# Mixing of the spectra in layer 4: one matmul per mode, real and imaginary weights side by side, in all eight PSUM banks

## Chip, cores and metric

The kernel runs on one core of a Trainium2 chip. The metric is the device time in microseconds (us) of one execution, lower is better. Three runs of the kernel before took 3917.05, 3924.25 and 3925.5 us; their median is 3924.25 us.

## The reference

Four layers are applied to x of shape (8, 32, 128, 128), batch by channel by height by width; each adds its result to its input after a per-plane normalisation `_gn`. The change is in the last layer, which multiplies a global transform by a 3x3 convolution with wrapped borders:

```
c_ft = rfft2(c)
top = einsum('bixy,ioxy->boxy', c_ft[:, :, :16, :16], w1)     # w1 = w1r + 1j*w1i
bot = einsum('bixy,ioxy->boxy', c_ft[:, :, -16:, :16], w2)    # w2 = w2r + 1j*w2i
out_ft = zeros; out_ft[:, :, :16, :16] = top; out_ft[:, :, -16:, :16] = bot
g = irfft2(out_ft);  l = conv3x3(c, wrap) + conv_b;  result = g * l
```

For each of the 512 kept modes (32 rows x by 16 columns y) there is a complex 32 by 32 matrix that turns the 32 input channels of each of 8 images into 32 output channels. This step is called the mixing here.

## The kernel before

Layers 1 to 3 fill most of the time, and the change leaves their work alone; only two semaphores of layer 1's batch norm (`bn_var`, `bn_sd`) are folded into two others with the same order of waits. Layer 4 is worked through image by image (index t, 0 to 7), each engine having its own list of instructions and waiting on counters of the others. For image t, ACT normalises, PE does the transform over rows (`dft_rows`, L789) and over columns (`dft_columns`, L801), ACT copies the spectrum from PSUM to the tile `cs` (`spectrum`, L1073, three copies: minus the imaginary part, the real part, the imaginary part), DVE transposes the image into bands (L1542) and PE convolves them (`conv`, L591, two halves per image of 288 PE matmuls each, into PSUM banks 0 to 3), and ACT copies the convolution out (`conv3_out`, L1080). Each float32 matmul of the program is two weight loads and two matmuls in the profile.

In `cs` and in the weight tile `wm`, partition quadrant q (32 partitions, one for each input channel) holds the modes with x = 4q to 4q+3 of either half of the spectrum. `mix_spectrum` (L857 to L868) does two matmuls per mode, each with 32 rows, 32 weight columns and 16 moving columns: the real weights times (real, imaginary), and the imaginary weights times (minus imaginary, real), added up in PSUM. Quadrant q of the input goes to quadrant q of PSUM, and `grp = (turn + q) % 4` gives the four quadrants a different one of the banks 4 to 7 at any time. There are 1024 such matmuls. The weights come by 16 DMAs of SP (L500), issued before the last image's bands are ready.

After `mix_spectrum` one count of `spec_mm` releases ACT, which copies the result out in 8 instructions (L1127) to the tile `ys`. PE meanwhile goes on with the convolution of the last image. SP waits for all 8 copies, stores `ys` by 8 DMAs (L545) and loads it back, transposed, by one (L548). After the last convolution half has been copied out, the final loop begins: for each image, a slice copy (ACT, L1135), the inverse transforms (PE, L887 and L898, with ACT's L1140 between), and DVE's product and sum (L1580, L1582); SP loads x and the convolution for it (L504, L311) and stores the result (L557). In SP's list `bands_out` (L488) stores a convolution half, `l3_in` and `x3_in` load for the final loop. Buffers for three images are there; the loads of the first three x and first two convolutions are issued before the mixing's results are waited for.

Of the kernel before, what the change touches and what calls it, by code (L numbers as in the profile page):

```python
# [7 lines left out]
ALU = mybir.AluOpType  # L8
ACT = mybir.ActivationFunctionType
AX = mybir.AxisListType  # L10

B, C, H, W = 8, 32, 128, 128
P = 128
# [8 lines left out]
NPX = CR * W  # L22
# [4 lines left out]
MODES = 16  # L27
KX = 2 * MODES
# [65 lines left out]
def after(eng, sem, n):  # L94

    if n > 0:
        eng.wait_ge(sem, n)


def four_layers(nc, x, conv0_w, conv0_b, bn_gamma, bn_beta, filt_x, filt_y, conv1_w, mix1_w, conv1_b, op_rows,  # L100
# [29 lines left out]
    with ExitStack() as ctx:  # L130
        def sb(name, shape, dt=F32):
            return ctx.enter_context(nc.sbuf_tensor(name, shape, dt))

        def once(name):

            return ctx.enter_context(nc.semaphore(name))
# [12 lines left out]
        k = sb("k", [P, NCONST])  # L149
# [17 lines left out]
        sd = sb("sd", [P, C])  # L167
        root = sb("root", [P, C])
        rstd = sb("rstd", [P, 4, C])
        nmr = sb("nmr", [P, 4, C])  # L170
        powers = sb("powers", [P, C])
# [17 lines left out]
        dog = sb("dog", [P, W + 2])  # L189
        cs = sb("cs", [P, 3, 2, 4, MODES, B])  # L190
        ps = ctx.enter_context(nc.psum_tensor("ps", [P, 8, NPX], F32))

        def part(at, n, rows=P):
            return arena[0:rows, at:at + n]
# [36 lines left out]

        wm = part(8192, 4 * C * 64).rearrange("p (r t o m) -> p r t o m", r=2, t=2, o=C)
        ys = part(37512, 2048).rearrange("p (a b m) -> p a b m", a=8, b=B)
# [30 lines left out]
        x_loaded, y_stored = two("x_loaded"), two("y_stored")  # L264
        bn_dev, bn_mat, bn_var, bn_sd, bn_ready = (once(n) for n in ("bn_dev", "bn_mat", "bn_var", "bn_sd", "bn_ready"))

# [21 lines left out]

        wm_loaded, spec_mm, spec_copy, spec_stored, spec_loaded = (once(n) for n in ("wm_loaded", "spec_mm", "spec_copy", "spec_stored", "spec_loaded"))
        xe_loaded, le_loaded, out_stored = ([sem(f"{n}{i}") for i in range(3)] for n in ("xe_loaded", "le_loaded", "out_stored"))  # L290
# [16 lines left out]
        def _(sp):  # L307
# [185 lines left out]
            def weights_in():  # L493

                sp.wait_ge(x3_stored[(B - 2) % 3], 16 * ((B - 2) // 3 + 1))
                sp.wait_ge(bands_ready, B - 1)
                sp.wait_ge(dfth_mm, 4 * (B - 1))
                for r, t, w in ((0, 0, w1r), (1, 0, w1i), (0, 1, w2r), (1, 1, w2i)):
                    for q in range(4):
                        sp.dma_start(wm[C * q:C * q + C, r, t, :, :],  # L500
                                     w[:, :, 4 * q:4 * q + 4, :].rearrange("i o x y -> i o (x y)")).then_inc(wm_loaded, 16)
# [38 lines left out]

            sp.wait_ge(spec_copy, 8)
            for t in range(2):
                for q in range(4):
                    first = MODES * t + 4 * q
                    sp.dma_start(spec_dram[first:first + 4].rearrange("x o m -> o x m"),  # L545
                                 ys[C * q:C * q + C, 4 * t:4 * t + 4, :, :].rearrange("p x b m -> p x (b m)")).then_inc(spec_stored, 16)
# [21 lines left out]
        def _(pe):  # L568
# [223 lines left out]
            def dft_columns(t):  # L792

                pe.wait_ge(dfth_copy, 4 * (t + 1))
                after(pe, dftw_copy, 3 * t)
                for half in range(2):
                    for xx in range(4):
                        for q in range(4):
                            for r in range(2):
                                at = 256 + (4 * half + xx) * 2 * MODES  # L800
                                m = pe.matmul(ps[C * q:C * q + C, 4, at:at + 2 * MODES], z[:, :, r, MODES * half + 4 * q + xx],  # L801
                                              dftw[:, r, :], start=r == 0, stop=r == 1)
                m.then_inc(dftw_mm, 1)
# [24 lines left out]
            for t in range(-2, B + 1):  # L828
# [5 lines left out]
                if 0 <= t < B:  # L834
                    after(pe, dftw_copy, 3 * t)
                    group_means(gn3, t)
# [21 lines left out]
            def mix_spectrum():  # L858

                for turn in range(4):  # L860
                    for m_ in range(KX):
                        for q in range(4):
                            grp = (turn + q) % 4
                            x8, ky = 2 * grp + m_ // MODES, m_ % MODES
                            t, xx = divmod(x8, 4)
                            for r in range(2):
                                m = pe.matmul(ps[C * q:C * q + C, 4 + grp, 16 * m_:16 * m_ + 16], wm[C * q:C * q + C, r, t, :, xx * MODES + ky],  # L867
                                              cs[C * q:C * q + C, 1 - r:3 - r, t, xx, ky, :], start=r == 0, stop=r == 1)  # L868
                m.then_inc(spec_mm, 1)

            pe.wait_ge(wm_loaded, 16 * 16)
            pe.wait_ge(dftw_copy, 3 * B)
            mix_spectrum()
            for half in range(HALVES):
                conv3(B - 1, half, range(TAPS))
# [26 lines left out]
        def _(act):  # L902
# [165 lines left out]
            def spectrum(t):  # L1068

                act.wait_ge(dftw_mm, t + 1)  # L1070
                sp_ = ps[:, 4, 256:256 + 8 * 2 * MODES].rearrange("p (x r y) -> p r x y", x=8, r=2)
                for n, (r, sign) in enumerate(((1, -1.0), (0, 1.0), (1, 1.0))):
                    nc.scalar.activation(cs[:, n, :, :, :, t:t + 1].rearrange("p t x y b -> p (t x) (y b)"),  # L1073
                                         sp_[:, r, :, :], ACT.Copy, scale=sign).then_inc(dftw_copy, 1)

# [47 lines left out]

            act.wait_ge(spec_mm, 1)
            for n in range(8):
                src = ps[:, 4 + n // 2, 256 * (n % 2):256 * (n % 2) + 256].rearrange("p (y r b) -> p b r y", y=MODES, r=2)
                nc.scalar.copy(ys[:, n, :, :].rearrange("p b (r y) -> p b r y", r=2), src).then_inc(spec_copy, 1)  # L1127

            for half in range(HALVES):
                conv3_out(B - 1, half)  # L1130
            act.wait_ge(spec_loaded, 16)
            act.wait_ge(spec_copy, 8)
            with act.Fori(0, B) as b:
# [14 lines left out]
        def _(pool):  # L1148
# [8 lines left out]
            for b in range(B):  # L1157
                pool.wait_ge(gn0.shifted, b + 1)
                nc.gpsimd.tensor_tensor(col0[:, 3:4], col0[:, 3:4], powers[:, 0:1], ALU.pow).then_inc(gn0.root, 1)  # L1159
            pool.wait_ge(bn_var, 1)  # L1160
            nc.gpsimd.tensor_tensor(root[:, :], sd[:, :], powers[:, :], ALU.pow).then_inc(bn_sd, 1)

# [57 lines left out]
        def _(dve):  # L1220
# [177 lines left out]
            t.inc(nc.vector.tensor_copy(bn_m[:, :], ps[:, 1, 0:2 * C]))  # L1398
            nc.vector.tensor_scalar(sd[:, :], ps[:, 1, C:2 * C], BN_EPS, None, ALU.add).then_inc(bn_var, 1)
            dve.wait_ge(bn_sd, 1)  # L1400
            t.inc(nc.vector.tensor_tensor(bn_a[:, :], root[:, :], gam[:, 0:C], ALU.mult))
# [144 lines left out]
            for i in range(-2, B):  # L1546
# [19 lines left out]
                if i >= 0:  # L1566
                    bands(i)

            for b in range(B):
                x3, l3 = xe[b % 3], le[b % 3]  # L1570
# [107 lines left out]
```

## Time and profile before

| | |
|---|---|
| profiled execution: time, and its span | 3922.26 us, 3920.1 us |
| median of three runs | 3924.25 us |
| PE busy, weight loads busy | 3338.9 us (85%), 1184.0 us (30%) |
| DVE, ACT, POOL busy | 2855.7 us (73%), 1849.5 us (47%), 2341.5 us (60%) |
| mean granted TensorE clock | 0.924 |
| chain that ended last | PE 30%, POOL 29%, issue 28%, DVE 5%, ACT 4%, DMA 2% |

The span runs from the first to the last instruction; the time of the execution has some 2 us around it. A stretch is named by its two ends in us from the span's start. In a list of instructions in order of time a row has start, duration, engine, line and operation, the tiles written and read, the shape, a count, and in brackets the idle time before it and what ended it. "Issue" is time in which an engine waited for nothing that the profile shows. Layer 4's images end and the mixing begins at 3640 us; the final loop begins at 3744 us.

### The profile page before, as it was taken

What the parts mean: (1) busy time and instruction counts of PE and PEld (TensorE: products, weight loads), DVE (VectorE), ACT (ScalarE), POOL (GpSimd) and SP (SyncE); (2) the same over time, 40 slices, a digit from 0 to 9 for tenths busy, and PEclk for the clock granted to TensorE, in tenths of its full rate; (3) what the DMA queues carried; (4) which work ended last, traced back from release to release, by engine and by line L of the source; (5) the groups of instructions that cost most, each with busy time, mean ns of one, the idle gap of its engine ahead of it and who ended that gap; (6) DMA issues with size and microseconds to landing.
All of it is one profiled execution on the core that took longest, in us unless ns stands there. A gap on an engine that the chain in (4) does not pass through costs nothing.

```text
span 3920.1 us, 89862 instructions
## 1 busy us (share of the span) xinstructions
PE 3338.9 (85%) x32900; PEld 1184.0 (30%) x32900; DVE 2855.7 (73%) x3513; ACT 1849.5 (47%) x2702; POOL 2341.5 (60%) x1131
## 2 busy tenths in 40 slices
PE   4678999759999999999999999999999957787565
PEld 2343444312212212222222222222222245555454
DVE  3652544469989989989989989989999956655034
ACT  0114566355545545555555555555555455665011
POOL 0000000049999999999999999999999923321000
PEclk9899999879999999999999999999999967888665
DMA  6574898566656656666666666666666664535589
GB/s 158 120 167 99 164 196 169 124 164 155 154 133 148 153 139 145 158 141 144 150 149 143 145 152 147 141 149 151 141 149 159 141 152 118 154 101 128 140 191 251
DMA packets 495204, 586.47 MB, mean 150 GB/s; under 512 B 71970, under 2 KB 334754, under 8 KB 489435
## 3 DMA queue, kind: packets, MB, share of 16 engines
q1 hardware_dynamic: 484212, 563.65, 62.5%
q10 hardware_dynamic: 10560, 16.93, 1.8%
q8 instruction: 287, 4.70, 0.5%
q14 instruction: 145, 1.19, 0.1%
HBM read 409.91 MB, written 184.54 MB: 152 GB/s over the span
## 4 chain that ended last, share of the span: by engine, by line
PE 30%; POOL 29%; issue 28%; DVE 5%; ACT 4%; DMA 2%; SPq 1%; ACTq 0%; POOLq 0%; DVEq 0%
POOL arena L1183 27%; PE ps L591 8%; PE ps L632 7%; PE ps L639 4%; PE ps L703 3%; POOL arena L1171 2%; ACT arena L936 2%; PE ps L789 1%; PE ps L811 1%; DVE arena L1542 1%; PE ps L685 1%; PE ps L898 1%; PE ps L867 1%; DMA arena<-x_dram 1%; DMA w_conv<-in_conv_w 1%
## 5 line engine op out<-in xcount | busy, mean ns | idle before, releaser
L1183 POOL TENSOR_TENSOR arena<-arena 128x1024 f32<-128x1024 f32 x896 | 1931.0, 2196 | 556.2 <-ACT arena L1039 556.2
L1494 DVE TENSOR_TENSOR arena<-ps,arena 128x1024 f32<-128x1024 f32 x1792 | 2107.4, 1220 | 204.9 <-PE ps L685 174.3
L703 PE MATMUL ps<-arena,w_mix 128*32 128x512 f32 x10752 | 1438.5, 607 | 79.4 <-POOL arena L1183 79.4
L1039 ACT ACTIVATE arena<-ps 128x1024 f32<-128x1024 f32 x896 | 918.9, 1026 | 1026.3 <-PE ps L695 1015.3
L685 PE MATMUL ps<-arena,sel 48*128 48x512 bf16 x3584 | 702.5, 385 | 24.8 <-issue 16.1
L685 PEld LDWEIGHTS ps<-arena,sel 48*128 48x128 bf16 x3584 | 190.1, 93 | 945.5 <-issue 936.8
L591 PE MATMUL ps<-arena,w_conv 32*32 32x512 f32 x9216 | 354.0, 650 | 42.6 <-issue 34.3
L695 PE MATMUL ps<-norms,opw 57*128 57x512 bf16 x1792 | 348.1, 384 | 49.2 <-ACT arena L971 17.5
L703 PEld LDWEIGHTS ps<-arena,w_mix 128*32 128x32 f32 x10752 | 214.3, 108 | 467.5 <-issue 467.5
L936 ACT ACTIVATE arena<-arena,nmr,rstd 128x128 f32<-128x128 f32 x768 | 300.5, 481 | 33.0 <-DVE arena L1544 30.4
L632 PE MATMUL ps<-arena,circ 128*128 128x512 f32 x640 | 287.9, 595 | 14.1 <-ACT arena L950 14.1
L695 PEld LDWEIGHTS ps<-norms,opw 57*128 57x128 bf16 x1792 | 101.8, 93 | 435.3 <-issue 430.0
L591 PEld LDWEIGHTS ps<-arena,w_conv 32*32 32x32 f32 x9216 | 179.1, 107 | 178.8 <-issue 125.5
L1215 POOL COPY arena<-arena 32x130 f32<-32x130 f32 x32 | 33.8, 1057 | 327.7 <-DVE arena L1544 326.7
L1166 POOL TENSOR_TENSOR arena<-arena 128x1024 f32<-128x1024 f32 x62 | 133.0, 2145 | 95.7 <-ACT arena L980 95.7
L1580 DVE TENSOR_TENSOR arena<-arena,ps 128x512 f32<-128x512 f32 x64 | 43.7, 683 | 192.7 <-PE ps L898 163.3
L639 PE MATMUL ps<-arena,circ 128*128 128x512 f32 x384 | 176.3, 594 | 0.0
L632 PEld LDWEIGHTS ps<-arena,circ 128*128 128x128 f32 x640 | 120.3, 189 | 166.6 <-issue 166.6
L1226 DVE BATCH_NORM_STATS2 st<-arena 128x6 f32<-128x128 f32 x768 | 156.5, 278 | 7.1 <-POOL arena L1202 4.9
L1422 DVE TENSOR_TENSOR arena<-arena 128x512 f32<-128x512 f32 x64 | 44.3, 692 | 143.1 <-ACT arena L955 141.1
L1159 POOL TENSOR_TENSOR col<-col,powers 128x1 f32<-128x1 f32 x8 | 4.4, 549 | 241.1 <-DVE col L1282 241.1
L811 PE MATMUL ps<-arena,ident 128*128 128x128 f32 x512 | 78.8, 319 | 70.0 <-ACT arena L936 69.9
(151 smaller groups left out, 2195.2 us busy)
## 6 DMA issues: line engine op xcount, KB each, us to landing
arena<-pad SPq DMA_DIRECT2D x768, 260.0 KB, 7.7
split_dram<-arena SPq DMA_DIRECT2D x64, 768.0 KB, 3.6
arena<-split_dram SPq DMA_DIRECT2D x1536, 32.0 KB, 3.2
x_dram<-arena SPq DMA_DIRECT2D x16, 2048.0 KB, 7.8
l_dram<-arena SPq DMA_DIRECT2D x128, 256.0 KB, 4.2
arena<-l_dram SPq DMA_DIRECT2D x32, 1024.0 KB, 14.1
arena<-x_dram SPq DMA_DIRECT2D x16, 2048.0 KB, 16.4
pad<-arena SPq DMA_DIRECT2D x8, 2080.0 KB, 16.4
```

The lines of the kernel that those rows point to most:

```text
L591: m = pe.matmul(ps[C * j:C * j + C, bank + g, :], weights[C * g:C * g + C, dy, dx, :], tile[C * g:C * g + C, r:r + CR, dx:dx + W], start=t ...
L632: m = pe.matmul(ps[:, n % 2, :], circ[:, d, :], yp[h % 2][:, 4 * n:4 * n + 4, 4 - d:4 - d + W], start=d == 0, stop=d == 4)
L639: m = pe.matmul(ps[:, 2 + n % 2, :], circ[:, 5 + d, :], yp[h % 2][:, 4 * n:4 * n + 4, 4 - d:4 - d + W], start=d == 0, stop=d == 2)
L685: m = pe.matmul(ps[:, 2 * (n % 2) + e, :], sel[ROWS2 * e:ROWS2 * e + SPLIT_ROWS, u % GROUP, :], split[ROWS2 * e:ROWS2 * e + SPLIT_ROWS, pa ...
L695: m = pe.matmul(ps[:, POOL_BANK + e, :], opw[ROWS2 * e:ROWS2 * e + KROWS, SPREAD[c], :], norms[ROWS2 * e:ROWS2 * e + KROWS, buf, half, :]. ...
L703: m = pe.matmul(ps[C * g:C * g + C, SUM + chunk % 2, :], w_mix[:, s, :], ring[:, (first + g // 2) % size, NPX * (g % 2):NPX * (g % 2) + NP ...
L936: m = nc.scalar.activation(tile[:, c, :], src[:, c, :], ACT.Identity, scale=rstd[:, gn.slot + n % 2, c:c + 1], bias=nmr[:, gn.slot + n % 2 ...
L1039: nc.scalar.activation(ring_p[:, slot, :], ps[:, POOL_BANK:POOL_BANK + 2, :].rearrange("p a n -> p (a n)"), ACT.Tanh).then_inc(tanh_p, 1)
L1166: nc.gpsimd.tensor_tensor(rest, tt, hml[:, 0, :], ALU.subtract).then_inc(rows_r, 1)
L1183: nc.gpsimd.tensor_tensor(slot, slot, pixels(chunk % 2, SPREAD[n // 2], n % 2), ALU.mult).then_inc(prod_p, 1)
L1226: m = nc.vector.bn_stats(st[:, c, :], tile[:, c, :])
L1494: nc.vector.tensor_tensor(slot, weights, pixels(par, ONCE[n // 2], n % 2), ALU.mult).then_inc(prod_d, 1)
```

## The change

Each mode gets one matmul: 32 rows, 64 weight columns (32 real, 32 imaginary, beside each other in `wm`), 16 moving columns (real and imaginary of 8 images). So 512 matmuls instead of 1024. The results are products, not yet combined: in a PSUM region of 64 partitions the lower 32 hold real weight times (real, imaginary), the upper 32 imaginary weight times the same. Quadrants 0 and 1 of the input go to partitions 0 to 63 and 64 to 127 of bank grp, quadrants 2 and 3 to those of bank 4+grp, so that all eight banks are filled. PE therefore waits for the evacuation of the convolution before (`conv3_evac` 14) ahead of the mixing, and for all combinations (`spec_copy` 4) behind it, ahead of the last image's convolution. The modes are done in four groups (quarters), with one count of `spec_mm` each. A quarter behind, ACT copies the imaginary-weight half to a new tile `crossed` (four copies of 32 partitions by 512 per group), and DVE combines it with the real-weight half from PSUM (eight instructions of 32 partitions by 256 elements per group) into `ys`. SP stores the first half of the spectrum after two groups, the second after four. `cs` loses its negated part, so that `spectrum` is two copies for each image.

```diff
-        cs = sb("cs", [P, 3, 2, 4, MODES, B])
+        cs = sb("cs", [P, 2, 2, 4, MODES, B])
+        crossed = sb("crossed", [P, 2, NPX])
-        wm = part(8192, 4 * C * 64).rearrange("p (r t o m) -> p r t o m", r=2, t=2, o=C)
+        wm = part(8192, 4 * C * 64).rearrange("p (t k m) -> p t k m", t=2, k=2 * C)
@@ SP @@
-                        sp.dma_start(wm[C * q:C * q + C, r, t, :, :],
+                        sp.dma_start(wm[C * q:C * q + C, t, C * r:C * r + C, :],
-            sp.wait_ge(spec_copy, 8)
             for t in range(2):
+                sp.wait_ge(spec_copy, 2 * t + 2)
                 for q in range(4):
@@ PE (dftw_copy is waited for at 2 * t instead of 3 * t) @@
-                for turn in range(4):
+                for grp in range(4):
                     for m_ in range(KX):
+                        x8, ky = 2 * grp + m_ // MODES, m_ % MODES
+                        t, xx = divmod(x8, 4)
                         for q in range(4):
-                            grp = (turn + q) % 4
-                            x8, ky = 2 * grp + m_ // MODES, m_ % MODES
-                            t, xx = divmod(x8, 4)
-                            for r in range(2):
-                                m = pe.matmul(ps[C * q:C * q + C, 4 + grp, 16 * m_:16 * m_ + 16], wm[C * q:C * q + C, r, t, :, xx * MODES + ky],
-                                              cs[C * q:C * q + C, 1 - r:3 - r, t, xx, ky, :], start=r == 0, stop=r == 1)
-                m.then_inc(spec_mm, 1)
+                            rows, at = slice(C * q, C * q + C), 2 * C * (q % 2)
+                            m = pe.matmul(ps[at:at + 2 * C, 4 * (q // 2) + grp, 16 * m_:16 * m_ + 16], wm[rows, t, :, xx * MODES + ky],
+                                          cs[rows, :, t, xx, ky, :], start=True, stop=True)
+                    m.then_inc(spec_mm, 1)
             pe.wait_ge(wm_loaded, 16 * 16)
-            pe.wait_ge(dftw_copy, 3 * B)
+            pe.wait_ge(dftw_copy, 2 * B)
+            pe.wait_ge(conv3_evac, 2 * (B - 1))
             mix_spectrum()
+            pe.wait_ge(spec_copy, 4)
             for half in range(HALVES):
                 conv3(B - 1, half, range(TAPS))
@@ ACT @@
-                for n, (r, sign) in enumerate(((1, -1.0), (0, 1.0), (1, 1.0))):
-                    nc.scalar.activation(cs[:, n, :, :, :, t:t + 1].rearrange("p t x y b -> p (t x) (y b)"),
-                                         sp_[:, r, :, :], ACT.Copy, scale=sign).then_inc(dftw_copy, 1)
+                for r in range(2):
+                    nc.scalar.activation(cs[:, r, :, :, :, t:t + 1].rearrange("p t x y b -> p (t x) (y b)"),
+                                         sp_[:, r, :, :], ACT.Copy).then_inc(dftw_copy, 1)
-            act.wait_ge(spec_mm, 1)
-            for n in range(8):
-                src = ps[:, 4 + n // 2, 256 * (n % 2):256 * (n % 2) + 256].rearrange("p (y r b) -> p b r y", y=MODES, r=2)
-                nc.scalar.copy(ys[:, n, :, :].rearrange("p b (r y) -> p b r y", r=2), src).then_inc(spec_copy, 1)
+            for grp in range(4):
+                act.wait_ge(spec_mm, grp + 1)
+                after(act, spec_copy, grp - 1)
+                for q in range(4):
+                    at = 2 * C * (q % 2) + C
+                    m = nc.scalar.copy(crossed[C * q:C * q + C, grp % 2, :], ps[at:at + C, 4 * (q // 2) + grp, :])
+                m.then_inc(spec_cross, 1)
             act.wait_ge(spec_loaded, 16)
-            act.wait_ge(spec_copy, 8)
@@ DVE, behind its work for the images and ahead of the final loop @@
+            for grp in range(4):
+                dve.wait_ge(spec_cross, grp + 1)
+                for q in range(4):
+                    at = 2 * C * (q % 2)
+                    real, imag = (tile.rearrange("p (x y r b) -> p r x b y", x=2, r=2, b=B)
+                                  for tile in (ps[at:at + C, 4 * (q // 2) + grp, :], crossed[C * q:C * q + C, grp % 2, :]))
+                    own = ys[C * q:C * q + C, 2 * grp:2 * grp + 2, :, :]
+                    nc.vector.tensor_tensor(own[:, :, :, 0:MODES], real[:, 0], imag[:, 1], ALU.subtract)
+                    m = nc.vector.tensor_tensor(own[:, :, :, MODES:KX], real[:, 1], imag[:, 0], ALU.add)
+                m.then_inc(spec_copy, 1)
```

Not shown: the renamed semaphores of layer 1, where POOL waits for `gn0.shifted` and DVE for `gn0.root` instead of `bn_var` and `bn_sd`.

## Rows read from the trace of the kernel before

**Rows 1.** Engines by stretch: length, busy us (count) of each, granted clock, DMA share, GB/s.

```profile
core 0: us, PE busy (x) PEld busy (x) DVE busy (x) ACT busy (x) POOL busy (x), PEclk, DMA share, GB/s
3650.00:3700.00 50.00, 20.18 (x1271) 19.11 (x1264) 0.00 (x0) 0.00 (x0) 0.00 (x0) 0.50 0.55 178
...
3840.00:3860.00 20.00, 14.48 (x192) 12.94 (x192) 9.16 (x15) 3.07 (x5) 0.00 (x0) 0.50 1.12 288
```

**Rows 2.** The chain that ended last, 3636 to 3752, its shares by line.

```profile
by line: issue 40.1%; PE ps L867 28.4%; PE ps L591 23.1%; PE ps L887 5.7%; ACT arena L1080 2.0%; ACT arena L1135 0.8%; ACTq L1133 0.1%; ACTq L1135 0.1%; ACTq L1137 0.0%; ACTq L1138 0.0%
```

**Rows 3.** Instructions in order of time, PE and its weight loads in the mixing.

```profile
3639.90 0.43 PEld L867 LDWEIGHTS ps<-cs,arena 32*32 32x32 f32 x9
...
3640.64 1.18 PEld L867 LDWEIGHTS ps<-cs,arena 32*32 32x32 f32 x69 [0.30 <-issue]
...
3648.28 2.05 PE L867 MATMUL ps<-cs,arena 32*32 32x16 f32 x128 [6.36 <-issue]
...
3657.78 2.05 PE L867 MATMUL ps<-cs,arena 32*32 32x16 f32 x128 [7.45 <-issue]
...
3679.89 2.05 PE L867 MATMUL ps<-cs,arena 32*32 32x16 f32 x128 [1.70 <-issue]
...
3687.10 2.05 PE L867 MATMUL ps<-cs,arena 32*32 32x16 f32 x128 [1.70 <-issue]
...
3716.51 0.83 PE L867 MATMUL ps<-cs,arena 32*32 32x16 f32 x43 [1.42 <-issue]
...
3717.29 11.42 PE L591 MATMUL ps<-arena,w_conv 32*32 32x512 f32 x280
```

**Rows 4.** DMA queues, 3676 to 3719: packets, MB, share of 16 engines.

```profile
q8 instruction: 12, 0.20, 2.0%
```

**Rows 5.** All instructions of L867: form, count, ns min/median/max, first and last start.

```profile
L867 PE MATMUL ps<-cs,arena x2048: 173/212/237, 3639.9 to 3717.3; 32*32 32x16 f32 x187
```

**Rows 6.** Instructions in order of time, on both sides of the mixing.

```profile
3606.95 5.58 PE L591 MATMUL ps<-arena,w_conv 32*32 32x512 f32 x96
...
3614.39 3.41 PE L591 MATMUL ps<-arena,w_conv 32*32 32x512 f32 x96
...
3640.91 2.12 ACT L1080 ACTIVATE arena<-ps,bias 128x1024 f32<-128x1024 f32 x2 [10.18 <-PE ps L591]
...
3717.52 2.31 ACT L1127 COPY arena<-ps 128x256 f32<-128x256 f32 x8 [74.49 <-PE ps L867]
...
3719.86 4.75 SPq L545 DMA_DIRECT2D spec_dram<-arena  x8
...
3744.23 1.03 ACT L1135 COPY arena<-arena 32x1024 f32 x1
3745.50 7.05 PE L887 MATMUL ps<-k,arena 32*32 32x128 f32 x128 [3.32 <-ACT arena L1135]
3749.19 1.07 ACT L1140 COPY arena<-ps 128x512 f32<-128x512 f32 x2 [3.94 <-PE ps L887]
3751.37 2.88 SPq L311 DMA_DIRECT2D arena<-l_dram  x2
3752.47 3.39 PE L898 MATMUL ps<-k,arena 64*128 64x128 f32 x32
```

**Rows 7.** All instructions of two lines of VectorE, columns as in Rows 5.

```profile
L1232 DVE COPY mu<-ps x24: 184/192/193, 368.9 to 3604.7; 128x32 f32<-128x32 f32 x24
...
L1580 DVE TENSOR_TENSOR arena<-arena,ps x64: 679/682/690, 3756.0 to 3909.5; 128x512 f32<-128x512 f32 x64
```

**Rows 8.** DMA issues, 3540 to the end: count, KB each, median us to landing.

```profile
spec_dram<-arena SPq DMA_DIRECT2D x8, 128.0 KB, 2.5
arena<-spec_dram SPq DMA_DIRECT2D x1, 1024.0 KB, 7.5
```

**Rows 9.** Instructions in order of time, around one image's spectrum copies.

```profile
3525.76 0.88 ACT L1073 ACTIVATE cs<-ps 128x128 f32<-128x128 f32 x3 [0.25 <-PE ps L801]
3531.75 12.44 ACT L936 ACTIVATE arena<-arena,nmr,rstd 128x128 f32<-128x128 f32 x32 [5.11 <-DVE arena L1544]
```

More of the change, by code:

```diff
@@ L264, in four_layers @@
         x_loaded, y_stored = two("x_loaded"), two("y_stored")
-        bn_dev, bn_mat, bn_var, bn_sd, bn_ready = (once(n) for n in ("bn_dev", "bn_mat", "bn_var", "bn_sd", "bn_ready"))
+        bn_dev, bn_mat, bn_ready = (once(n) for n in ("bn_dev", "bn_mat", "bn_ready"))
         xt_loaded, yt_loaded, x1_stored, xn1_stored, parts_stored, rows_stored = (two(n) for n in (
@@ L287, in four_layers @@
             "bands_ready", "halo_ready", "dfth_mm", "dfth_copy", "dftw_mm", "dftw_copy", "conv3_mm", "conv3_evac"))
-        wm_loaded, spec_mm, spec_copy, spec_stored, spec_loaded = (once(n) for n in ("wm_loaded", "spec_mm", "spec_copy", "spec_stored", "spec_loaded"))
+        wm_loaded, spec_mm, spec_cross, spec_copy, spec_stored, spec_loaded = (once(n) for n in (
+            "wm_loaded", "spec_mm", "spec_cross", "spec_copy", "spec_stored", "spec_loaded"))
         xe_loaded, le_loaded, out_stored = ([sem(f"{n}{i}") for i in range(3)] for n in ("xe_loaded", "le_loaded", "out_stored"))
@@ L794, in dft_columns @@
                 pe.wait_ge(dfth_copy, 4 * (t + 1))
-                after(pe, dftw_copy, 3 * t)
+                after(pe, dftw_copy, 2 * t)
                 for half in range(2):
@@ L834, in _ @@
                 if 0 <= t < B:
-                    after(pe, dftw_copy, 3 * t)
+                    after(pe, dftw_copy, 2 * t)
                     group_means(gn3, t)
@@ L1159, in _ @@
                 nc.gpsimd.tensor_tensor(col0[:, 3:4], col0[:, 3:4], powers[:, 0:1], ALU.pow).then_inc(gn0.root, 1)
-            pool.wait_ge(bn_var, 1)
-            nc.gpsimd.tensor_tensor(root[:, :], sd[:, :], powers[:, :], ALU.pow).then_inc(bn_sd, 1)
+            pool.wait_ge(gn0.shifted, B + 1)
+            nc.gpsimd.tensor_tensor(root[:, :], sd[:, :], powers[:, :], ALU.pow).then_inc(gn0.root, 1)
             def rows_rest(b, chunk):
@@ L1398, in _ @@
             t.inc(nc.vector.tensor_copy(bn_m[:, :], ps[:, 1, 0:2 * C]))
-            nc.vector.tensor_scalar(sd[:, :], ps[:, 1, C:2 * C], BN_EPS, None, ALU.add).then_inc(bn_var, 1)
-            dve.wait_ge(bn_sd, 1)
+            nc.vector.tensor_scalar(sd[:, :], ps[:, 1, C:2 * C], BN_EPS, None, ALU.add).then_inc(gn0.shifted, 1)
+            dve.wait_ge(gn0.root, B + 1)
             t.inc(nc.vector.tensor_tensor(bn_a[:, :], root[:, :], gam[:, 0:C], ALU.mult))
```

## The prediction

> **What bounds the kernel now.** I first read the engines by stretch. Between 3650 and 3700 us PE is busy for 20.18 of 50 us, at the lower clock level (0.50), and DVE, ACT and POOL do nothing at all [rows 1]: the mixing is a stretch of its own, with nothing beside it but DMAs. The chain of waits from 3636 to 3752 says the same: 40.1% of it is "issue", 28.4% is L867, 23.1% the convolution L591 [rows 2]. So what shortens the mixing shortens the kernel, unless a transfer takes over.
>
> Then the order of time. L867 has 2048 PE matmuls (two for each of the program's 1024) and as many weight loads [rows 5]. They come in bursts: 9+69 = 78 at the start, then fifteen of 128 and a last one of 50. A burst of 128 takes 2.05 us, so 16.0 ns for a pair of load and matmul, and is followed by idle time put down to "issue": 6.36 and 7.45 us early, 1.70 or 1.42 us late [rows 3]. 128 pairs are 256 instructions, and in the 43 us from 3676 to 3719 the instruction queue moved 12 packets with 0.20 MB [rows 4], or 16.7 KB every 3.6 us: one packet for each burst, 65 bytes for each instruction. I read this as PE waiting for its own instructions. From 3676 on they come at a pitch of some 3.7 us (3679.89, 3687.10 two bursts later [rows 3]); while the loads for the final loop fill the DMA engines it is 6 to 9.5 us (3648.28 to 3657.78). The eighth burst starts at 3687.10, the sixteenth at 3716.51 [rows 3].
>
> A rule speaks against that reading: the Trainium skill (Runtime: NRT & Kernel Launch, Instruction fetch mechanics) says that a refill is mostly hidden, since instructions are dispatched slower than blocks arrive. By it the mixing would cost its busy 16 x 2.05 = 33 us, half of it would be saved, and after the new wait and tail little more than 8 us would be left. The idle time behind every burst contradicts it here, and the sum goes by the trace.
>
> **The change part by part.**
> *Pairs.* 512 program matmuls are 1024 pairs instead of 2048. If bursts arrive when they did, 78 + 7x128 + 50 pairs are needed: the last 50 are in the eighth burst, at 3687.10. The loads that slow the early bursts are issued ahead of the mixing's results and stay where they are.
> *Price of a pair.* No row has 32 rows by 64 weight columns. Below: 16.0 ns as now. Above: L898 (64 rows by 128 columns, twice the weights and 128 moving columns) has 32 pairs in 3.39 us, 106 ns [rows 6]. The nearest row is L867 itself: same rows, same 16 moving columns, same clock. Four row groups share the 16.0 ns, so 64 ns for each; doubled, that is 32 ns a pair. I take 24 ns, 3.1 us for 128: still inside the pitch of 3.7 us, so only the last 50 cost more. End of the mixing: 3687.10 + 50 x 0.024 + 0.2 (a matmul's 212 ns [rows 5]) = 3688.5.
> *New wait ahead.* ACT's evacuation ends at 3640.91 + 2.12 = 3643.0 [rows 6]; the first 78 pairs start there instead of at 3639.9. The next burst came only at 3648.28, so this 3.1 us costs nothing. Without that cover (if instructions were never late) it would be 3.1 us. Behind the wait on PE stand only the mixing and the last convolution.
> *Order by quarter.* Group 2 is complete after 768 pairs, in the burst that starts at 3679.89. ACT's four copies: 0.54 us each by L1140 (two in 1.07 us [rows 6]), 2.2 us. DVE's eight instructions have 256 elements. L1232 has 32 in 0.19 us, L1580 512 in 0.68 us [rows 7], and the line between gives 0.42; below 0.19, above 0.68. Eight are 3.3 us (1.5 to 5.5). The third group's 5.5 us end near 3686, before the fourth is ready: three tails are hidden, one is on the path.
> *Tail.* 3688.5 + 2.2 + 3.3 + 0.2 for two hand-overs = 3694.2. There PE begins the last convolution, which began at 3717.3 [rows 3]. New on the path: 5.7 us in which PE waits, where it now goes on at once and ACT's 2.31 us (L1127 [rows 6]) lie beside it.
> *Clock.* Now the convolution starts at the lower level and its first half takes 11.42 us [rows 3]. After a pause it may stay there longer: 96 matmuls took 5.58 us at 3606.95 against 3.41 at 3614.39 [rows 6]. Bounds 0 and 2.2 us, I take 0.4: most of that loss is already in today's 11.42.
> *Store and load of the spectrum.* Half is stored before; the last four stores start at 3694.2 (SP issued eight in 4.75 us [rows 6], so 2.4), land 2.5 us later, the load takes 7.5 [rows 8]: 3707. It is needed by L1135, behind the convolution: 3744.2 now, 3721 then. Hidden with 14 us to spare. SP's new wait for two groups has nothing urgent behind it.
> *Final loop.* Its first load (L311 at 3751.37 [rows 6]) waits for the stored convolution, and each later one for a product of the loop; so the whole loop moves with its start, though later its DMA share is 1.12 [rows 1].
> *Spectrum copies.* One fewer of three in 0.88 us for each image; ACT then waits 5.11 us for DVE's bands [rows 9]. Nothing. The renamed semaphores of layer 1: same order, nothing.
>
> Sum: 3717.3 - 3694.2 - 0.4 = 22.7 us. The profiled execution took 3922.26 us (span 3920.1 and 2.2 around it), which gives 3899.6. The median of the runs lies 2.0 above it: 3901.6 us. My own range for this case is 3897 to 3907 (pairs from 16 to 32 ns, DVE from 0.19 to 0.68, clock).
>
> **The rivals.**
> *B, quadrants wait for each other in one bank.* Today `grp` keeps four row groups in four banks; now quadrants 0 and 1 write halves of the same bank, and 2 and 3 too. If PE lets the second in only when the first's 212 ns [rows 5] are over, every four matmuls cost 2 x 212: 53 ns a pair, 6.8 us a burst. Bursts then queue up: with starts 3657.78, 3664.6 and so on each 6.8 later, the eighth starts at 3698.6 and ends at 3701.3; tail and clock as above, the convolution starts at 3707.4. Gain 10 us, 3914. For it: the care that the code takes today, and no row with two row groups in one bank. Against: the two use different partitions. The Trainium skill (TensorEngine Tiling, Restrictions and Gotchas) states that different row tiles cannot use the same PSUM bank at one time; if that includes separate partitions, this rival or the next is the outcome. No row of this trace shows it.
> *C, slower.* The mechanism is the weight load: 64 columns wide, no longer overlapped from one row group to the next, so that every pair costs what L898's does, 106 ns. 1024 pairs from 3643.0 are 108.5 us, the convolution starts at 3757.6 with the tail and 0.4: 40 us late, 3964. It decides against the change from (3717.3 - 6.1 - 3643.0)/1024 = 67 ns a pair. Against it: today's loads do overlap (16 ns a pair), and L898 has 128 moving columns to explain its 106.
> *D, larger gain.* Instructions flow on during PE's waits, the bursts stop marking the time, and the tail is short: the last pair near 3684, DVE at its lower bound. Gain 26 to 29 us, 3897. Against: the pitch is the same whatever PE does between bursts.
> *E, given back.* The final loop runs into its DMAs (1.12 [rows 1]) and ends no earlier: 3924. It needs a transfer that doesn't hang on the loop's start, and I find none.
> *F, a dear tail.* DVE or ACT pays for reading one quadrant and writing another with strides, at twice the price for all four groups: the third group's 11 us then delay the fourth, and 8 to 11 us are lost. 3911.
>
> **Chances.** Forecast 0.60, B 0.13, C 0.08, D 0.07, E 0.05, F 0.07. A change within 0.2% (8 us, about what a measurement of this kernel can tell from none) is E and the part of B where the loss is larger than its price: 0.07. Faster is the forecast, the rest of B, D and F: 0.85. Slower is C: 0.08. The range for 8 in 10 takes in forecast, D, F and most of B, and leaves out C and E: 3895 to 3916.
>
> **What would show it.** Right: L867's successor has 1024 matmuls, bursts of 128 with "issue" behind them, starts as now, the last pair near 3688; DVE's last combination near 3694; the load of the spectrum long done when the final loop starts, near 3722. B shows as bursts of some 6.8 us, C of 13.6. A burst that starts later than its counterpart says that the fetch hangs on PE's progress more than I assume. If the mixing ends as forecast and the end doesn't move, it is E. The forecast is wrong if the last convolution starts after 3703 or before 3689.

## The result, and the profile after

The changed kernel took 3903.78 us (median of five runs, 3895.24 to 3910.16) against 3924.25 us before; the ratio is 0.9949 with a 95% interval of 0.9931 to 0.9967. That is 20.5 us less. The profiled execution of after took 3895.24 us (span 3893.1), the fastest of the five; against the profiled one of before, 3922.26 us, it is 27.0 us.

The stretch that answers to [rows 1] (same columns):

```profile
3650.00:3700.00 50.00, 29.36 (x956) 26.13 (x960) 16.91 (x32) 9.23 (x16) 0.00 (x0) 0.53 0.72 213
```

PE is busy longer (29.36 us for 20.18), and DVE and ACT now work beside it. The order of time in the mixing and behind it, which answers to [rows 3] and [rows 6] (L868 is the new matmul, L1132 ACT's copy, L1580 and L1581 DVE's two combinations, L593 the convolution, L547 and L550 the spectrum's store and load, L1139 the first slice of the final loop):

```profile
3643.22 5.91 PE L868 MATMUL ps<-cs,arena 32*64 32x16 f32 x206 [2.30 <-ACT arena L1083]
...
3655.04 3.72 PE L868 MATMUL ps<-cs,arena 32*64 32x16 f32 x128 [5.90 <-issue]
...
3659.88 3.72 PE L868 MATMUL ps<-cs,arena 32*64 32x16 f32 x128 [1.12 <-issue]
...
3666.91 3.72 PE L868 MATMUL ps<-cs,arena 32*64 32x16 f32 x128 [3.31 <-issue]
...
3672.85 3.72 PE L868 MATMUL ps<-cs,arena 32*64 32x16 f32 x128 [2.22 <-issue]
...
3678.79 8.77 PE L868 MATMUL ps<-cs,arena 32*64 32x16 f32 x306 [2.22 <-issue]
...
3687.59 2.34 ACT L1132 COPY crossed<-ps 32x512 f32<-32x512 f32 x4 [4.70 <-PE ps L868]
3689.97 0.56 DVE L1580 TENSOR_TENSOR arena<-ps,crossed 32x256 f32<-32x256 f32 x1 [2.78 <-ACT crossed L1132]
...
3693.66 0.57 DVE L1581 TENSOR_TENSOR arena<-ps,crossed 32x256 f32<-32x256 f32 x1
...
3694.29 11.53 PE L593 MATMUL ps<-arena,w_conv 32*32 32x512 f32 x288 [6.73 <-DVE arena L1581]
...
3697.82 0.32 SPq L550 DMA_DIRECT2D arena<-spec_dram  x1
...
3708.02 10.59 PE L593 MATMUL ps<-arena,w_conv 32*32 32x512 f32 x288 [2.21 <-ACT arena L1083]
...
3720.66 1.03 ACT L1139 COPY arena<-arena 32x1024 f32 x1
```

1024 pairs in bursts of multiples of 128 (the first is 78 + 128), 3.72 us for 128; idle time put down to issue between them while the loads for the final loop run; from 3678.79 on, 306 pairs without a gap. The last pair ends at 3687.6, the last convolution starts at 3694.29, the final loop at 3720.66, where it was 3744.23 [rows 6]: 23.6 us earlier. The remaining 3.4 us of the profiled pair lie in the loop: it takes 172.4 us to the end of the span, and took 175.9.

In the experiments the work ahead of the mixing ends at different times from one execution to the next. With nothing edited ahead of it, the first matmul of the mixing starts anywhere from 3642.4 (e2) to 3653.2 us (e10); in e4 and e11, where loads are moved, it starts at 3635.7 and 3635.0. So the times scatter by more than many effects here, and stretches of the profile are compared. "Stage" is from the first matmul of the mixing to the first slice of the final loop, "loop" from there to the end of the span.

| kernel | stage | loop | time: median (profiled execution) |
|---|---|---|---|
| before | 104.3 | 175.9 | 3924.25 (3922.3) |
| changed | 77.4 | 172.4 | 3903.8 (3895.2) |
| changed, once more (e13) | 84.2 | 171.9 | 3900.8 (3902.8) |
| e1 four banks | 84.7 | 172.5 | 3900.0 |
| e2 one tail | 95.0 | 176.6 | 3914.9 |
| e3 half the pairs of before | 76.8 | 173.5 | 3889.5 |
| e4 loads late | 81.6 | 172.3 | 3891.8 (one run) |
| e5 loads early | 71.2 | 172.2 | 3892.6 |
| e6 by quadrant | 81.9 | 172.3 | 3904.3 (one run) |
| e7 early, by quadrant | 73.8 | 176.7 | 3895.9 |
| e9 eight columns | 84.0 | 176.2 | 3906.0 (one run) |
| e10 load behind half | 81.5 | 171.9 | 3904.2 |
| e11 early, by quadrant, held | 68.5 | 172.5 | 3885.4 |
| e12 early, by quadrant, x later | 71.9 | 175.0 | 3889.0 |

What sets the length of the loop can be read from the profiles. Each of its eight images begins with 128 matmuls of the same shape (L887, L890 in the changed kernel). For the second image, before and changed:

```profile
3764.45 7.05 PE L887 MATMUL ps<-k,arena 32*32 32x128 f32 x128
3741.27 3.85 PE L890 MATMUL ps<-k,arena 32*32 32x128 f32 x128
```

The granted clock over these two rows is 0.50 and 0.94. In all eight profiles with a loop of 171.9 to 172.5 us this second group took 3.8 to 4.2 us, and in all six with 173.5 to 176.7 us it took 7.05 us. The short loops have two or three of their eight groups at 6.9 us or more, e3 three, before four, the others five or six. So the length of the loop goes with TensorE's clock level in it, and with no edit that the runs tell of. What makes the clock rise earlier in one execution than in another is not shown.

### The profile page after: what moved, and what is told of

Its sections match the earlier page's. It is cut to its first block, busy times and chain, and to the rows that moved or that the text cites. A ratio compares the mean times of both kernels' runs of the same rounds, so it can differ in the third digit from the quotient of the medians.

```text
span 3893.1 us, 87847 instructions
## 1 busy us (share of the span) xinstructions
PE 3326.5 (85%) x31876; PEld 1174.5 (30%) x31876; DVE 2871.1 (74%) x3545; ACT 1853.3 (48%) x2702; POOL 2344.9 (60%) x1131
## 4 chain that ended last, share of the span: by engine, by line
POOL 30%; PE 29%; issue 28%; DVE 5%; ACT 4%; DMA 2%; SPq 1%; ACTq 0%; POOLq 0%; DVEq 0%
POOL arena L1187 27%; PE ps L593 8%; PE ps L634 7%; PE ps L641 4%; PE ps L705 3%; POOL arena L1175 2%; ACT arena L939 2%; PE ps L791 1%; PE ps L813 1%; DVE arena L1546 1%; PE ps L687 1%; PE ps L901 1%; DMA arena<-x_dram 1%; DVE arena L1595 1%; PE ps L868 1%
## 5 line engine op out<-in xcount | busy, mean ns | idle before, releaser
L593 PE MATMUL ps<-arena,w_conv 32*32 32x512 f32 x9216 | 350.2, 642 | 52.7 <-issue 34.8
L939 ACT ACTIVATE arena<-arena,nmr,rstd 128x128 f32<-128x128 f32 x768 | 300.5, 480 | 34.5 <-DVE arena L1548 31.8
L1219 POOL COPY arena<-arena 32x130 f32<-32x130 f32 x32 | 44.3, 1385 | 324.4 <-DVE arena L1548 323.4
L593 PEld LDWEIGHTS ps<-arena,w_conv 32*32 32x32 f32 x9216 | 176.0, 107 | 188.2 <-issue 124.0
L1426 DVE TENSOR_TENSOR arena<-arena 128x512 f32<-128x512 f32 x64 | 44.3, 692 | 143.1 <-ACT arena L958 141.2
L1175 POOL TENSOR_TENSOR arena<-arena 128x1024 bf16<-128x1024 f32 x62 | 133.1, 2146 | 0.0
```

The costliest lines, as they stand in the source:

```text
L593: m = pe.matmul(ps[C * j:C * j + C, bank + g, :], weights[C * g:C * g + C, dy, dx, :], tile[C * g:C * g + C, r:r + CR, dx:dx + W], start=t ...
L939: m = nc.scalar.activation(tile[:, c, :], src[:, c, :], ACT.Identity, scale=rstd[:, gn.slot + n % 2, c:c + 1], bias=nmr[:, gn.slot + n % 2 ...
L1175: nc.gpsimd.tensor_tensor(hml[:, 2, :], rest, hml[:, 1, :], ALU.subtract).then_inc(rows_l, 1)
```

## Experiments

### What paces the mixing, and what a pair costs

**Half the pairs of before (e3).** It leaves out the products of the imaginary weights.

```diff
-                            for r in range(2):
+                            for r in range(1):
                                 m = pe.matmul(ps[C * q:C * q + C, 4 + grp, ...],
-                                              ..., start=r == 0, stop=r == 1)
+                                              ..., start=True, stop=True)
```

> Kernel before, with the matmuls of the imaginary weights left out (the spectrum lacks their part): 512 matmuls of 32 weight columns, the instruction count of the changed kernel at the old price of a pair. Theory 1 (the mixing is paced by its instructions): bursts of 128 pairs in 2.05 us start at about the same times as before, the last 50 pairs in the eighth near 3687, the last convolution follows at once near 3688, 29 us earlier than before: 3895. Rival (paced by the array's work; idle time behind each burst is something else that follows the work): half of the busy 33 us goes, 3907 to 3909.

Time 3889.49 us, ratio 0.9902 (0.988 to 0.9925), and in order of time:

```profile
3680.19 2.01 PE L867 MATMUL ps<-cs,arena 32*32 32x16 f32 x128 [3.93 <-issue]
3683.94 2.01 PE L867 MATMUL ps<-cs,arena 32*32 32x16 f32 x128 [1.73 <-issue]
3687.68 2.02 PE L867 MATMUL ps<-cs,arena 32*32 32x16 f32 x128 [1.73 <-issue]
3691.43 0.80 PE L867 MATMUL ps<-cs,arena 32*32 32x16 f32 x42 [1.73 <-issue]
```

Same bursts, same price (2.01 us for 128), same idle time behind each, half as many. The stage is 27.5 us shorter; half of the busy time would have been 16. So before was paced by the number of its instructions. The rule that a refill is mostly hidden (the Trainium skill, Runtime: NRT & Kernel Launch, Instruction fetch mechanics) does not hold here: a burst of 2.01 us is followed by 1.73 to 7.49 us of waiting for the next. At equal instruction count, the changed kernel's wider pairs cost nothing that can be seen: from the first to the last pair of the mixing it took 44.3 us (45.7 in e13), and e3 49.2. What the changed kernel has on top is its tail, behind the last pair.

**Four banks at a time (e1)**, for rival B.

```diff
-  m = pe.matmul(ps[at:at + 2 * C, 4 * (q // 2) + grp, ...
+  m = pe.matmul(ps[at:at + 2 * C, 4 * (q // 2) + (grp + 2 * q) % 4, ...
```

The same index stands in ACT's copies and DVE's combinations.

> Changed kernel, but quadrants 1 and 3 write bank (grp + 2) % 4 of their set of four, so that the four quadrants are in four different banks at any time, as in the kernel before; everything else equal. Theory 1 (the 64-column weight load sets the 29 ns of a pair, not the shared bank): a burst of 128 pairs stays at 3.7 us (306 pairs 8.8 us), the last pair near 3687.5, time equal to the changed kernel's 3903.8 within 4 us. Rival (two row groups in one bank wait for each other): a burst falls to 2.1 to 2.6 us; the end of the mixing moves by only 1 to 2 us, since the instructions come every 3.7 us anyway. The burst decides, not the time.

**Eight columns (e9).** It leaves out the imaginary parts of the spectrum.

```diff
-  m = pe.matmul(ps[..., 16 * m_:16 * m_ + 16], ..., cs[rows, :, t, xx, ky, :], ...)
+  m = pe.matmul(ps[..., 16 * m_:16 * m_ + 8], ..., cs[rows, 0, t, xx, ky, :], ...)
```

> Changed kernel with 8 moving columns (real parts alone) for each mode instead of 16; half of the products are not computed. Theory 1 (weight load of 64 columns sets the pair): a burst of 128 pairs stays between 3.3 and 3.7 us. Rival (the moving columns and their writes to PSUM set it): it halves towards 1.9 to 2.4 us.

A burst of e1 and one of e9:

```profile
3670.69 3.72 PE L868 MATMUL ps<-cs,arena 32*64 32x16 f32 x128 [2.22 <-issue]
```

```profile
3670.86 3.70 PE L868 MATMUL ps<-cs,arena 32*64 32x8 f32 x128 [2.78 <-issue]
```

3.72 us with four banks, 3.72 with two, 3.70 with half the moving columns. Neither the bank nor the moving columns set the pair; e3's 2.01 us at the same 16 columns and same clock level (0.50) leaves the width of the weights: 32 columns 15.7 ns, 64 columns 29.1 ns. Wider weights also mean that 64 instead of 32 PSUM partitions are written; whether the loading or the writing takes the time was not tried apart. The rule that different row tiles cannot use one PSUM bank at a time (the Trainium skill, TensorEngine Tiling, Restrictions and Gotchas) doesn't bind here, where they write different partitions of it. The time of e1 was 3900.01 us, ratio 0.9927 (0.9907 to 0.9946): no different from the changed kernel's (3903.8 and 3900.8).

### What holds the bursts up

**Loads late (e4).**

```diff
+            bands_out(B - 2, 1)
+            sp.wait_ge(spec_mm, 4)
             l3_in(0)
             l3_in(1)
             ...
-            bands_out(B - 2, 1)
```

> Changed kernel, but the five loads for the final loop (two convolutions, three x, 10.5 MB) are issued only when the mixing is over; the store of image 6's convolution stays ahead. Theory 2 (the early bursts are late because their instruction packets queue behind these loads): bursts follow each other at 3.7 to 3.9 us from the start, 1024 pairs take 30 to 33 us and end near 3675, 12 us earlier; then the last convolution, with the loads beside it, is held up for instructions instead, by 3 to 10 us. Rival (packets are slow in that stretch for another reason, the DMAs before 3640 or PE's pause): idle times of 2 to 6 us stay between the first five bursts, end of the mixing near 3687.

```profile
3635.72 5.91 PE L869 MATMUL ps<-cs,arena 32*64 32x16 f32 x206 [2.30 <-ACT arena L1084]
3642.02 10.77 PE L869 MATMUL ps<-cs,arena 32*64 32x16 f32 x384 [0.39 <-issue]
...
3661.02 5.46 PE L869 MATMUL ps<-cs,arena 32*64 32x16 f32 x178 [0.30 <-issue]
...
3686.24 4.75 PE L594 MATMUL ps<-arena,w_conv 32*32 32x512 f32 x83 [4.05 <-issue]
...
3686.80 12.20 SPq L548 DMA_DIRECT2D spec_dram<-arena  x8
...
3717.36 1.04 ACT L1140 COPY arena<-arena 32x1024 f32 x1 [9.71 <-DMA arena<-spec_dram]
```

The mixing takes 30.8 us, without gaps to speak of, where it takes 44.3 with the loads beside it: they cost the changed kernel 13.5 us there. But it comes back: the convolution waits 4.05 us for instructions, and the spectrum's store is issued behind the loads, so that the final loop waits 9.71 us for the spectrum. Stage 81.6 us. The expectation had missed the second of these. The time, 3891.8 us, is one run, and its mixing began at 3635.7: that it is below the changed kernel's is not put down to the edit.

**Loads early (e5).** In the pass for image 6, when their buffers are free:

```diff
                 if t >= 2:
                     bands_out(t - 2, 1)
+                if t == B - 2:
+                    for half in range(2):
+                        sp.wait_ge(l3_stored[half], 64 * 2)
+                    sp.wait_ge(x2_done, 4 * (B - 1))
+                    l3_in(1)
+                    sp.wait_ge(x3_stored[(B - 3) % 3], 16 * ((B - 3) // 3 + 1))
+                    sp.wait_ge(gn3.out, 4 * (B - 2))
+                    l3_in(0)
 ... (and, behind the last image, with their waits:)
-            l3_in(0)
-            l3_in(1)
```

> Changed kernel, but the loads of the first two convolution images (4.2 MB of the 10.5) are issued one image earlier, near 3545, where the DMA engines have room; their buffers are free by then. Theory 2: the DMA engines are busy until about 3660 instead of 3676, so bursts wait only until then; the mixing ends near 3680 instead of 3687.6, and the time falls by 5 to 9 us, to 3896. Rival (the packets' pace there is not set by how much is loaded): end near 3687, time within 2 us of 3904.

```profile
3650.12 5.92 PE L871 MATMUL ps<-cs,arena 32*64 32x16 f32 x206 [2.30 <-ACT arena L1086]
...
3658.37 3.72 PE L871 MATMUL ps<-cs,arena 32*64 32x16 f32 x128 [2.34 <-issue]
...
3663.76 18.25 PE L871 MATMUL ps<-cs,arena 32*64 32x16 f32 x640 [1.67 <-issue]
...
3682.21 1.72 PE L871 MATMUL ps<-cs,arena 32*64 32x16 f32 x50 [0.20 <-issue]
```

The mixing takes 33.8 us (3650.1 to 3683.9), the stage 71.2. Time 3892.64 us, ratio 0.9917 (0.9901 to 0.9934).

### What the tails cost

**One tail (e2).**

```diff
-                act.wait_ge(spec_mm, grp + 1)
+                act.wait_ge(spec_mm, 4)
```

> Changed kernel, but ACT waits for all four groups before its first copy, so that nothing of ACT's and VectorE's work lies beside the mixing. Theory 1 (three of four tails are hidden behind PE, and the start of the last convolution sets the end): VectorE's four groups of 4.3 us follow each other after ACT's 2.3 us, 19.5 us where there are 6.7 now; the last convolution and the final loop start 13 us later, time 3917. Rival (the final loop's DMAs set the end, and its start has slack): the loop starts 13 us later, and the time is 3904 to 3908.

```profile
3675.73 9.21 PE L868 MATMUL ps<-cs,arena 32*64 32x16 f32 x306 [2.22 <-issue]
...
3704.54 8.99 PE L593 MATMUL ps<-arena,w_conv 32*32 32x512 f32 x205 [19.60 <-DVE arena L1581]
```

PE waits 19.60 us instead of 6.73. The time is 3914.85 us, ratio 0.9973 (0.9959 to 0.9987): working a quarter behind is worth 12.9 us in the profile and 11.1 between the medians, over half of what the change gained. It only just fits: in the changed kernel the third quarter's last combination ends at 3687.19 us (3686.62 and 0.57), 0.4 us before the last pair.

**By quadrant (e6).** One count of `spec_cross` for each copy, and in DVE's loop over q `dve.wait_ge(spec_cross, 4 * grp + q + 1)`.

> Changed kernel, but each of ACT's copies has its own count, and VectorE starts on quadrant 0 while ACT copies quadrant 1. Theory: from the last pair of the mixing to the start of the last convolution it takes 0.6 + 4.3 + 0.1 = 5.0 us instead of 6.7. Rival (ACT's and VectorE's reads of one bank slow each other): VectorE's instructions get longer than 0.57 us and less than 1 us is gained.

From the last group's first copy (ACT) to DVE's first combination and PE's convolution:

```profile
3693.76 2.38 ACT L1132 COPY crossed<-ps 32x512 f32<-32x512 f32 x4 [4.67 <-PE ps L868]
...
3694.37 0.56 DVE L1579 TENSOR_TENSOR arena<-ps,crossed 32x256 f32<-32x256 f32 x1 [2.77 <-ACT crossed L1132]
```

DVE starts 0.61 us behind ACT instead of 2.38, its instructions stay at 0.56 to 0.58 us, and PE's wait is 4.96 us instead of 6.73, here as in e7 and e12, which have the same edit. The 1.8 us are less than one run can tell in the time.

### A packet behind the spectrum's load

In e1, e2, e4, e5, e6 and e9 the first half of the last convolution is cut in two by an idle time which the first profile of the changed kernel doesn't have.

**The changed kernel once more (e13)**, unedited:

> The changed kernel once more, with nothing edited, for a second profiled execution of it. Theory 3 (its first profiled execution, 3895.2 us with a median of 3903.8, was one in which the packet came through ahead of the spectrum's load): this profile shows 2.5 to 3.5 us of issue time in the first half of the last convolution, a half of 14 to 17 us instead of 11.5, and 81 to 85 us from the first matmul of the mixing to the final loop instead of 77.5. Rival (the idle time in the edited kernels came from the edits): none, and 77 to 79 us.

```profile
3697.03 9.73 PE L593 MATMUL ps<-arena,w_conv 32*32 32x512 f32 x205 [6.72 <-DVE arena L1581]
3700.60 0.32 SPq L550 DMA_DIRECT2D arena<-spec_dram  x1
3709.20 4.79 PE L593 MATMUL ps<-arena,w_conv 32*32 32x512 f32 x83 [2.44 <-issue]
```

The instruction queue moved a packet at 3689 and the next at 3706; in the first profile there was one at 3699. The half takes 17.0 us (3697.03 to 3713.99) instead of 11.5. The stage is 84.2 us and not 77.4. So the edits had not brought it; the first profiled execution was one without it.

In e13 no packet moved from 3690 to 3706 us, though the DMA engines were idle until 3697. PE ran 205 matmuls of the convolution, 410 instructions with their weight loads, and then stood still; in all nine profiles with this idle time it comes behind 205 matmuls. So packets were not fetched further ahead while PE waited for the tail, and the next one met the spectrum's store and load. In the first profile that packet moved at 3699 us, 5 us into the convolution.

**Load behind half (e10).**

```diff
             sp.wait_ge(spec_stored, 16 * 8)
+            sp.wait_ge(conv3_mm, 2 * (B - 1) + 1)
```

> Changed kernel, but SP loads the spectrum back only when the first half of the last convolution is done on PE. Theory 3 (in most executions of the changed kernel one instruction packet of that half queues behind the spectrum's load, 2.7 to 3.4 us of issue time and a first half of 14 to 17 us where the profiled execution has 11.5): the first half takes 11.3 to 12.5 us; the load lands near 3716, ahead of its use near 3721, and may hold up a packet of the second half instead. Time 3899 to 3904 against the changed kernel's 3903.8. Rival (the stall comes from PE's pause ahead of the convolution, in which no packet is asked for): the first half keeps an idle time of 2 to 4 us with the load out of the way.

```profile
3706.09 12.20 PE L594 MATMUL ps<-arena,w_conv 32*32 32x512 f32 x288 [6.73 <-DVE arena L1582]
3718.33 2.12 ACT L1084 ACTIVATE arena<-ps,bias 128x1024 f32<-128x1024 f32 x2 [16.59 <-PE ps L594]
3718.37 0.32 SPq L551 DMA_DIRECT2D arena<-spec_dram  x1
3720.50 12.14 PE L594 MATMUL ps<-arena,w_conv 32*32 32x512 f32 x288 [2.21 <-ACT arena L1084]
```

No idle time in either half, with the same pause ahead of the convolution: the rival is excluded. From the start of the convolution to the loop it is 28.6 us, against 31.8 in e13 and 26.4 in the first profile. Part of what is won in the first half is lost in the second: that takes 12.14 us at a granted clock of 0.86 here, and 10.61 us at 1.00 in e13 (10.59 at 1.00 in the first profile). The time (3904.2 us, ratio 0.9946, 0.993 to 0.9963) shows no gain over the changed kernel's 3903.8 and 3900.8: this profile's mixing began at 3653.2 and took 46.1 us, so other differences between executions are as large.

### Together

e7 is e5 and e6, e11 adds e10, e12 is e7 with `x3_in(2)` moved behind `bands_out(B - 1, 0)`.

> Changed kernel with both edits that helped by themselves: the first two convolution images loaded one image earlier, and VectorE starting by quadrant. Theory: the gains add, since one lies ahead of the last pair and one behind it. From the first matmul of the mixing to the first slice of the final loop: 71.2 us with the early loads alone, less 1.7, so 69.5; time 3891 (3892.6 less 1.7), with the packet of the last convolution still behind the spectrum's load (idle time of about 3 us in its first half). Rival (the end is set by the DMAs of the final loop, so that an earlier start no longer counts): the stretch shortens, and the loop takes as much longer than its 172 us.

> The same, and the spectrum is loaded back only behind the first half of the last convolution. Theory 3: the idle time of about 3 us in that half, and the slow clock that follows it, go: 66 to 68 us from the first matmul of the mixing to the final loop, 2 to 3 us less than without holding the load, time 3888 to 3890. Rival (a packet of the second half takes the delay over): the stretch stays at 69 to 70 us.

> Early loads and VectorE by quadrant, and x of the third image is loaded behind the first half of the last convolution, not in the mixing (the load of the spectrum isn't held). Theory 2: 2.1 MB less beside the mixing, which gets 2 to 4 us shorter (1024 pairs in 31 to 33 us, which is what the pairs cost by themselves); against it the loads that now follow are later by some 8 us, which the final loop, short of DMA time, gives back in part. Time 3888 to 3892. Rival (the loop's DMAs decide): 3895 or more, with a loop of 176 us or more.

e7: 3895.86 us, ratio 0.9928 (0.9910 to 0.9946), stage 73.8 where 69.5 was expected: the gains did not add in this execution; its convolution's first half took 18.3 us with the packet late (5.90 us for its last 83 matmuls). e11: 3885.35 us, ratio 0.9906 (0.9891 to 0.9921), stage 68.5. e12: 3888.98 us, ratio 0.9911 (0.9898 to 0.9925), stage 71.9; its mixing is the shortest of the three (33.5 us, e7 35.0, e11 34.7), but its loop took 175.0 us, so that neither its theory nor the rival stands clear of the scatter. The profile of e11:

```profile
3649.15 14.41 PE L872 MATMUL ps<-cs,arena 32*64 32x16 f32 x512 [1.67 <-issue]
3664.40 5.24 PE L872 MATMUL ps<-cs,arena 32*64 32x16 f32 x178 [0.85 <-issue]
3674.60 12.35 PE L597 MATMUL ps<-arena,w_conv 32*32 32x512 f32 x288 [4.95 <-DVE arena L1584]
3689.16 12.23 PE L597 MATMUL ps<-arena,w_conv 32*32 32x512 f32 x288 [2.21 <-ACT arena L1087]
```

Between e7 and e11 lie 10.5 us of the medians, on one chip, more than the 2 to 3 expected. The two profiled executions differ by 17.0: 7.4 because the mixing of e11 began earlier, with the same work ahead of it, 4.2 by a shorter loop, which goes with the clock level as said above, and 5.3 in the stage. Only the last can be put down to the held load. From the start of the last convolution to the loop e11 takes 28.8 us, against 33.9 in e7 and 33.4 in e12. In the time the gain is not shown: the six runs of e7 (3883.0 to 3903.2) and of e11 (3877.0 to 3889.5) overlap, and e12, which does not hold the load, has a median only 3.6 us above e11's. e11 has the lowest median of the versions that compute the whole layer: 18.4 us below the changed kernel's (another chip), 35 below the runs of before beside it (3920.4). Its slowest run is faster than the fastest of either kernel.

## Why the prediction was right

The time forecast was 3901.6 us, the measured median 3903.8. The mechanism held: the mixing was paced by its instruction packets, and half as many instructions shortened it. That the total came within 2.2 us is in part luck, because two things that the sum did not have work against each other. By the forecast the stage is 78.5 us (3643.0 to 3721.5). In e13 it is 84.2, since a packet of the convolution is late; but its loop is 4.0 us shorter than before, which goes with the clock. The terms, on the profiled execution:

- *Last pair*: forecast 3688.5, measured 3687.6. Two differences cancel. A pair costs 28.7 to 29.1 ns, not 24; it is near the upper of my two values, 32. The packets came otherwise than assumed: the second packet was there by the end of PE's wait, so that 206 pairs ran at once where I had 78, and the packet behind it came at 3655.04, not at 3657.78 as in [rows 3]. In the late part a burst (3.72 us) now fills the whole pitch of its packets, so the mixing stands at both bounds at once. "If bursts arrive when they did" was the weak assumption, and it cost little.
- *Tail*: forecast 5.7 us, measured 6.73. DVE's term was mis-sized. A combination of 32 partitions by 256 takes 0.56 to 0.57 us and eight take 4.3 us, not 3.3. The line through a copy of 32 and a product of 512 elements [rows 7] gave 0.42; it left out what these operands add (strided, from PSUM and another quadrant), and no experiment says which of them it is. Copies: 2.34, not 2.2.
- *Start of the last convolution*: 3694.2 forecast, 3694.29 measured: the two errors above cancel, and this is luck, not precision.
- *New wait ahead*: no cost, as forecast. *Three tails hidden*: e2 shows it, 12.9 us; the third took 6.6 us, not 5.5, and just fitted.
- *Clock*: forecast 0.4 us lost; the first half took 11.53 us (11.42 [rows 3]), the second 10.59, where it was 11.25. Nothing was lost in this execution. In e10 and e11, also without a late packet, the two halves together took 24.3 and 24.6 us, 1.7 and 1.9 more than before: inside my bounds of 0 to 2.2, so the 0.4 stands for a term that varies from one execution to the next.
- *Store and load of the spectrum*: I called it hidden with 14 us to spare. For the data that is so. But its traffic was priced by its landing alone, and not by what is behind it in the DMA engines: PE's next instruction packet. This was late in nine of the ten profiles that have the new tail and don't hold the load back (all but the first of the changed kernel; in e4 the late loads were there as well), and the first half then takes 15.3 to 18.3 us instead of 11.5. e10 and e11 move only the load behind the half, the store stays where it was, and neither has the idle time; so the store by itself does not delay the packet, and the load is needed for it. This is the step that was wrong, the same effect that I had read in the early bursts and did not carry over to here. The first profiled execution did not have it; in e13, which did, the shorter loop makes up for most of it.
- *Final loop*: moves with its start (E excluded). Its length is 171.9 to 172.5 us in some profiles and 173.5 to 176.7 in others, before included. It goes with the clock level, 0.50 or 0.94 over the second image's matmuls, which the sum took as unchanged; what sets the level is not shown, so the 3.4 us of the first pair of profiles is not put down to the change.
- Rivals: B excluded by e1, C by the pair's 29 ns (it decides from 67), D and F not seen as such, though F's direction was right for DVE (4.3 for 3.3 us, not twice). B's 53 ns counts two pairs for each matmul of the program in its 212 ns; if each pair waited by itself it would be 106 ns, and e1 excludes both.
- The "little more than 8 us" that would be gained if PE never waited for packets was not worked through: half of 33 us less a wait of 3.1 and a tail of 5.7 is 7.7, and with pairs of 24 ns instead of 16 nothing would be left. The idle time behind each burst spoke against that case, and e3 bears this out.

## What to carry to other kernels

A long run of small matmuls can wait for its own instructions: look for bursts of equal count with idle time that has no releaser, and compare them with the packets of the instruction queue. There the number of instructions is the price, and so is every bulk transfer beside them; move transfers to where PE's instructions last long. When a transfer is called hidden, ask also whose instruction packet it delays.

## What the hardware showed

- The instruction queue moved one packet for each 256 instructions of PE. In the mixing of before the bursts began every 3.5 to 4.0 us with the DMA engines idle, and up to 9.5 us apart with five large loads queued [rows 3, 4].
- In e13 no packet moved for 16 us, across PE's wait for the tail and the start of the convolution, of which 410 instructions ran before PE stood still.
- 128 matmuls of the loop's first kind took 7.05 us at a granted clock of 0.50 and 3.85 us at 0.94. The loops in which more images had the slower ones took up to 176.7 us, the others 172.
- With 32 rows and four row groups in turn, at the lower clock level, a pair of weight load and matmul took 16 ns with 32 weight columns and 28 to 29 ns with 64, and the same 29 with 8 or 16 moving columns, in two banks or four.
- DVE took 0.57 us for 32 partitions by 256 float32 elements, with one operand in PSUM and one in another tile; 512 elements on 128 partitions take 0.68 [rows 7].
